# A recommendation tower on one Trainium2 core: the last chunk's late stage in two parts of two tiles

## The reference

```python
e = jnp.stack([tbl_0[ids[:, 0]], tbl_1[ids[:, 1]], ..., tbl_25[ids[:, 25]]], axis=1)   # (2048, 26, 128)
sd = jnp.einsum('bfd,bd->bf', sparse_values, dense_features)
ss = jnp.einsum('bfd,bgd->bfg', sparse_values, sparse_values)
pairs = ss[:, iu, ju]                                   # 325 pairs above the diagonal
z = jnp.concatenate([dense_features, sd, pairs], axis=1)
h = jnp.concatenate([z, r_dense_features], axis=1)      # 607 wide
h = jnp.maximum(h @ W_top1 + b_top1, 0.0)               # 512
h = jnp.maximum(h @ W_top2 + b_top2, 0.0)               # 256
y = h @ W_top3                                          # (2048, 1)
```

## Time and profile before

| what | value |
|---|---|
| median of three runs | 391.6 us (390.85 to 392.52) |
| the profiled execution | 391.02 us |
| its span, first to last instruction | 389.2 us |
| busy: PE, PE weight loads | 348.4 us (90%), 269.9 us (69%) |
| busy: DVE, ACT, POOL | 242.9, 190.6, 264.3 us |
| mean granted clock of TensorE | 0.952 |

### The profile page before, as it was taken

One profiled execution on the slowest core, in us unless ns is written; L12 is line 12 of the kernel. 1 busy time (PEld: TensorE's weight loads), 2 busy tenths in 40 slices (PEclk: granted clock), 3 DMA queues, 4 the chain that ended last, 5 costly groups with the idle time before them and its releaser, 6 DMA issues.

```text
span 389.2 us, 12471 instructions
## 1 busy us (share of the span) xinstructions
PE 348.4 (90%) x5471; PEld 269.9 (69%) x5471; DVE 242.9 (62%) x475; ACT 190.6 (49%) x299; POOL 264.3 (68%) x279
## 2 busy tenths in 40 slices
PE   2899985999999999999999989999999988346996
PEld 0566664877788877777788878776788876235773
DVE  0789996877888644887987446886986341101420
ACT  3356664768323337577143157674133169822333
POOL 6777775777777777777777777777777777771000
PEclk9999998999999998999999998999999989756899
DMA  7999212333333232343223222433431222220000
GB/s 189 247 233 216 49 47 93 89 86 88 112 85 81 83 74 62 90 99 105 85 84 105 78 61 52 117 90 90 110 80 54 54 56 58 57 53 20 3 0 0
DMA packets 20107, 33.41 MB, mean 86 GB/s; under 512 B 7916, under 2 KB 10488, under 8 KB 20055
## 3 DMA queue, kind: packets, MB, share of 16 engines
q0 software_dynamic: 8704, 17.84, 18.2%
q1 hardware_dynamic: 11351, 14.78, 14.3%
HBM read 32.60 MB, written 0.01 MB: 84 GB/s over the span
## 4 chain that ended last, share of the span: by engine, by line
PE 37%; POOL 8%; issue 4%; ACT 3%; DMA 1%; DVE 1%; POOLq 0%; ACTq 0%; DVEq 0%
PE late_bank L599 9%; POOL rows L498 8%; PE gram_bank L561 5%; PE turn_bank L542 3%; PE turn_bank L522 3%; PE turn_bank L523 3%; PE late_bank L522 2%; PE late_bank L523 2%; PE spare_bank L635 2%; ACT turned L349 2%; DMA rows<-in_tbl_dram,index 1%; PE gram_bank L635 1%; PE turn_bank L579 1%; PE late_bank L647 1%; PE gram_bank L579 1%
## 5 line engine op out<-in xcount | busy, mean ns | idle before, releaser
L498 POOL DMA_INDIRECT rows<-in_tbl_dram,index x272 | 263.5, 969 | 87.1 <-issue 79.5
L915 DVE TENSOR_TENSOR one_hot<-table_ids,row_number 125x512 fp32r<-125x512 int32 x216 | 134.4, 682 | 27.3 <-PE turn_bank L523 15.4
L349 ACT COPY turned<-turn_bank 128x512 f32<-128x512 f32 (+1 forms) x72 | 70.9, 1029 | 47.1 <-PE turn_bank L542 47.0
L542 PE MATMUL turn_bank<-ident,rows 128*128 128x128 f32 x288 | 48.2, 302 | 21.2 <-DMA rows<-in_tbl_dram,index 11.2
L522 PE MATMUL late_bank<-one_hot,table_hi 125*128 125x512 f32 x144 | 61.8, 429 | 0.9 <-DVE table_lo L996 0.9
L561 PEld LDWEIGHTS gram_bank<-turned 128*27 128x27 f32 x4096 | 46.9, 110 | 22.4 <-issue 19.9
L561 PE MATMUL gram_bank<-turned 128*27 128x26 f32 x4096 | 56.2, 197 | 5.8 <-issue 5.3
L542 PEld LDWEIGHTS turn_bank<-ident,rows 128*128 128x128 f32 x288 | 36.9, 155 | 31.4 <-issue 16.6
L523 PE MATMUL late_bank<-one_hot,table_lo 125*128 125x512 f32 x144 | 58.3, 405 | 0.0
L319 DVE COPY gram<-gram_bank 124x208 f32<-124x208 f32 x32 | 12.0, 374 | 59.3 <-PE gram_bank L561 59.0
L522 PE MATMUL turn_bank<-one_hot,table_hi 125*128 125x512 f32 x96 | 38.8, 404 | 1.0 <-DVE one_hot L913 1.0
(11 more groups left out here) (84 smaller groups left out, 400.9 us busy)
## 6 DMA issues: line engine op xcount, KB each, us to landing
table_ids<-in_ids_by_table_dram SPq DMA_DIRECT2D x27, 256.0 KB, 3.3
rows<-in_tbl_dram,index POOLq DMA_INDIRECT x272
turned<-in_tbl_dram SPq DMA_DIRECT2D x6, 448.0 KB, 13.7
looked_up<-in_tbl_dram SPq DMA_DIRECT2D x3, 448.0 KB, 6.5
rows<-in_r_dense_features_dram SPq DMA_DIRECT2D x16, 64.0 KB
gram<-in_W_top_dram SPq DMA_DIRECT2D x1, 702.0 KB
gram<-in_W_top_dram SPq DMA_DIRECT2D x1, 512.0 KB
turned<-in_tbl_dram SPq DMA_DIRECT2D x6, 52.0 KB
```

The source lines that it names most:

```text
L349: copy(to[:, f0:f1], of).then_inc(rows_copied[n % 2], 1)
L498: pool.indirect_dma_start(out=rows[:, row % RING_ROWS, :], out_offset=None, in_=tables[f], in_offset=bass.IndirectOffsetOnAxis(ap=index[:, ...
L542: last = pe.transpose(turn_bank[n % 2][:, f - f0, :], rows[:, (tile * ROWS + f) % RING_ROWS, :], ident[:])
L915: last = nc.vector.tensor_tensor(hot, table_ids[0:RK, (chunk.n * LOOKUPS + s) % ID_SLOTS, 0:wide], row_number[0:RK, k:k + 1].broadcast_to( ...
```

## The change

The last chunk's late stage is done in two parts, `EARLY` with tiles 12 and 13 and `FINAL` with tiles 14 and 15, each with 256 samples as its moving columns where there were 512. The number of instructions of the late stage doubles with that. `EARLY` is written between the products of tile 14 and the turns of tile 15. So that both can be in flight, `EARLY` has PSUM banks of its own (the spare bank, the bank of the row numbers, a late bank) and its own room for pairs and for `h2` in the half of `gram` that tiles 14 and 15 no longer need, since their products go where those of tiles 12 and 13 were. In the last chunk the odd row turns are copied by DVE and the even ones by ACT, where ACT copied all of them, and DVE places the looked-up rows of tiles 14 and 15. The output is stored in two parts. Chunks 0 to 2 keep their order. The core of the diff:

```diff
+EARLY = Part(LAST.n, LAST.first, HALF, 0)
+FINAL = Part(LAST.n + 1, LAST.first + HALF, HALF, HALF)
+PARTS = len(CHUNKS) + 1
...
+        half_room = HALF * GROUPS * LATER
+        early_pairs_room = late_room[:, half_room:half_room + GROUP * PAIRS]
+        half_h2 = late_room[:, half_room:half_room + N2 * HALF * P].rearrange("p (n b) -> p n b", n=N2)
+        last_y = late_room[0:1, half_room + N2 * HALF * P:half_room + N2 * HALF * P + CHUNK]
...
+        half_cols_bank = [spare_bank[:], row_number[:], late_bank[1][:], *free_bank[0:2], spare_bank[:], row_number[:]]
+        whole_pairs_bank = free_bank
+        half_pairs_bank = [bank[:, 0:HALF * P] for bank in (gram_bank[1], spare_bank, row_number)]
...
+        half_h2_bank = [spare_bank[:], row_number[:]]
...
+            room = n % (HALF * UNITS) if chunk is LAST else n
+            copy(gram[0:ACROSS, room * UNIT:(room + 1) * UNIT, :], of).then_inc(gram_copied[mine], 1)
...
+                if part.tiles == TILES:
+                    if g == 2 and part is not LAST:
+                        pe.wait_ge(found_copied, (part.n + 2) * LOOKUPS + LATE - 2)
+                    if g >= COLS_TURNS - 2:
+                        pe.wait_ge(cols_copied[0], part.n * COLS_STEPS[0] + g - (COLS_TURNS - 2) + 1)
+                else:
+                    if g == 0:
+                        pe.wait_ge(y_rows_copied, 1)
+                    if g >= COLS_TURNS - 2:
+                        pe.wait_ge(cols_copied[g - (COLS_TURNS - 2)], part.n * COLS_STEPS[g - (COLS_TURNS - 2)] + 1)
...
+                elif n == 1:
+                    pe.wait_ge(cols_copied[0], part.n * COLS_STEPS[0] + 2)
...
+            def work_off_last():
+                for t in range(HALF):
+                    for u in range(UNITS):
+                        turn_rows(LAST, t + 1, turns_before(u))
+                        products(LAST, t, u)
+                    if t == 0:
+                        turn_outputs()
+                turn_rows(LAST, 3, (0,))
+                dense_ahead(EARLY, 0)
+                for g in range(COLS_TURNS):
+                    turn_products(EARLY, g)
+                pe.wait_ge(cols_copied[1], EARLY.n * COLS_STEPS[1] + 2)
+                products(LAST, 2, 0)
+                for k in range(K_PAIRS):
+                    turn_pairs(EARLY, k)
+                turn_rows(LAST, 3, (1,))
+                pe.wait_ge(pairs_split, EARLY.n * K_PAIRS + 1)
+                products(LAST, 2, 1)
+                dense_ahead(EARLY, 1)
+                layer1(EARLY, 0)
+                turn_rows(LAST, 3, (2,))
+                layer1(EARLY, 1)
+                products(LAST, 2, 2)
+                layer2(EARLY, 0)
+                layer1(EARLY, 2)
+                turn_rows(LAST, 3, (3,))
+                products(LAST, 2, 3)
+                layer2(EARLY, 1)
+                layer1(EARLY, 3)
+                layer2(EARLY, 2)
+                layer2(EARLY, 3)
+                turn_rows(LAST, 3, (4,))
+                half_layer3(EARLY)
+                for u in range(UNITS):
+                    products(LAST, 3, u)
+                dense_ahead(FINAL, 0)
+                for g in range(COLS_TURNS):
+                    turn_products(FINAL, g)
+                for k in range(K_PAIRS):
+                    turn_pairs(FINAL, k)
+                dense_ahead(FINAL, 1)
+                for n in range(N1):
+                    layer1(FINAL, n)
+                    for k in LAYER2_AFTER[n]:
+                        layer2(FINAL, k)
+                layer2(FINAL, N1 - 1)
+                half_layer3(FINAL)
...
+            def work_off_last():
+                for t in range(HALF):
+                    for u in range(UNITS):
+                        copy_rows(act, LAST, t + 1, [g for g in turns_before(u) if g % 2 == 0])
+                        if u % 2:
+                            copy_products(act, LAST, t * UNITS + u)
+                        if u == 1 and t == 0:
+                            place_found(act, LAST, 1)
+                    if t == 0:
+                        copy_output_rows()
+                copy_rows(act, LAST, 3, (0,))
+                for g in range(1, COLS_TURNS, 2):
+                    copy_cols(act, EARLY, g)
+                for k in range(K_PAIRS):
+                    copy_pairs(EARLY, k)
+                copy_products(act, LAST, 2 * UNITS + 1)
+                relu1(EARLY, 0)
+                copy_rows(act, LAST, 3, (2,))
+                relu1(EARLY, 1)
+                relu1(EARLY, 2)
+                copy_products(act, LAST, 2 * UNITS + 3)
+                relu1(EARLY, 3)
+                for n in range(N2):
+                    relu2(EARLY, n)
+                copy_rows(act, LAST, 3, (4,))
+                copy_output(EARLY)
+                for u in range(1, UNITS, 2):
+                    copy_products(act, LAST, 3 * UNITS + u)
+                for g in range(1, COLS_TURNS, 2):
+                    copy_cols(act, FINAL, g)
+                for k in range(K_PAIRS):
+                    copy_pairs(FINAL, k)
+                for n in range(N1):
+                    relu1(FINAL, n)
+                for n in range(N2):
+                    relu2(FINAL, n)
+                copy_output(FINAL)
...
+            def work_off_last():
+                for t in range(HALF):
+                    for u in range(UNITS):
+                        copy_rows(dve, LAST, t + 1, [g for g in turns_before(u) if g % 2])
+                        if u % 2 == 0:
+                            copy_products(dve, LAST, t * UNITS + u)
+                        if u == 1 and t == 1:
+                            place_found(dve, LAST, 2)
+                    split_dense(LAST, t)
+                for g in range(0, COLS_TURNS, 2):
+                    copy_cols(dve, EARLY, g)
+                copy_products(dve, LAST, 2 * UNITS)
+                for k in range(K_PAIRS):
+                    split_pairs(EARLY, k)
+                copy_rows(dve, LAST, 3, (1,))
+                place_found(dve, LAST, 3)
+                split_h1(EARLY, 0)
+                split_h1(EARLY, 1)
+                copy_products(dve, LAST, 2 * UNITS + 2)
+                split_h1(EARLY, 2)
+                copy_rows(dve, LAST, 3, (3,))
+                split_dense(LAST, 2)
+                split_h1(EARLY, 3)
+                copy_products(dve, LAST, 3 * UNITS)
+                split_dense(LAST, 3)
+                copy_products(dve, LAST, 3 * UNITS + 2)
+                for g in range(0, COLS_TURNS, 2):
+                    copy_cols(dve, FINAL, g)
+                for k in range(K_PAIRS):
+                    split_pairs(FINAL, k)
+                for n in range(N1):
+                    split_h1(FINAL, n)
```

More of the change, by code:

```diff
@@ L52 @@
 TILES = 4
-SIZES = (4, 4, 4, 4)
+CHUNK_COUNT = 4
+HALF = TILES // 2
 CHUNK = TILES * P
@@ L98, with width, groups_in, samples_of @@
 SPREAD = 112
[L101 to L118, removed]
+Part = namedtuple("Part", "n first tiles at")
+CHUNKS = [Part(n, n * TILES, TILES, 0) for n in range(CHUNK_COUNT)]
+LAST = CHUNKS[-1]
+EARLY = Part(LAST.n, LAST.first, HALF, 0)
+FINAL = Part(LAST.n + 1, LAST.first + HALF, HALF, HALF)
+PARTS = len(CHUNKS) + 1
+def width(part):
+    return part.tiles * P
+def groups_in(part):
+    return part.tiles * GROUPS
+def samples_of(part):
+    return slice(part.at * P, (part.at + part.tiles) * P)
 def offset(row):
@@ L140, in turns_until, with blocks_before, blocks_after, hots_after @@
     return row // ROWS * TURNS + row % ROWS // TURN + 1
[L143 to L157, removed]
+def blocks_before(step):
+    return sum(BLOCKS.get(before, 0) for before in STEPS[:STEPS.index(step)])
+def blocks_after(*step):
+    return range(blocks_before(step), blocks_before(step) + BLOCKS.get(step, 0))
+def hots_after(*step):
+    blocks = blocks_after(*step)
     first = 0 if step == ("unit", 0, 0) else min(blocks.start + HOT_SLOTS, HOTS)
@@ L593, in turn_pairs, with add_layer1 @@
                 last.then_inc(pairs_turned, 1)
-            def add_layer1(chunk, n, k):
-                p, cols, wide = height(k), slice(n * P, (n + 1) * P), width(chunk)
+            def add_layer1(part, n, k):
+                p, cols = height(k), slice(n * P, (n + 1) * P)
                 for w, x in ((w1_hi, input_hi), (w1_hi, input_lo), (w1_lo, input_hi)):
-                    last = pe.matmul(h1_bank[n][:, 0:wide], w[0:p, k, cols], x[0:p, k, 0:wide],
+                    last = pe.matmul(h1_bank[n][:, 0:width(part)], w[0:p, k, cols], x[0:p, k, samples_of(part)],
@@ L658, in last_layer3, with turn_outputs @@
                 last.then_inc(y_summed, 1)
[L660 to L662 removed]
+            def turn_outputs():
+                pe.wait_ge(y_copied, LAST.n + 1)
                 pe.transpose(y_rows_bank, y[:], ident[:]).then_inc(y_turned, 1)
             def work_off(chunk, following):
[L668 to L671 removed]
+                for t in range(TILES):
@@ L799, in copy_output @@
                 else:
```

(6 more changed lines are left out.)

329 lines of the change are left out of this document (142 added, 187 removed).

## The result

The changed kernel takes 385.74 us, the median of six runs (383.97 to 387.31), where the kernel before took 391.77 (390.85 to 393.29, six runs beside them). The ratio is 0.9839, with an interval from 0.9803 to 0.9875: 1.6% faster. The forecast was 387.0, in a range from 383.0 to 391.5. The profiled execution took 384.49 us.

The account below looks back on a forecast made before the run. A gather-bound stretch with PE mostly idle, then 28.9 us of full PE work. The final part saves 9.7 us, 5.2 given back before it: span 384.7, 4.5 less; profiled execution 386.5, forecast 387.0, range 383.0 to 391.5.

Parts of the forecast that it names:

- The gather-bound stretch is filled: Tile 15's gathers: last stays at 351, early work fills PE's idle time, clock full from about 343.
- Tile 15's products start late by 5.2 us, at 360.5: Early part on PE, from 337.57: its work pushes the start of tile 15's products from 355.30 to 360.5.
- The wait for the fourth block: Early part, layer one's fourth block: PE idles 0.8 us for two ACT instructions and one on DVE.
- 256 columns at 0.127 us: Half-wide float32r matmuls: 0.107 of streaming plus 0.02 per instruction; bounds 0.117 and 0.233; 141 on the path.
- the rival that drew on such a sum: Half-wide matmuls over 0.15 us each; at 0.237, with weight loads not hidden, 402 us. Chance 0.14, no gain at all 0.03.
- Column turns with 64 weight columns at 0.075: Column turns of each half: 0.075 us each, between 0.06 and 0.117, and 0.15 at low clock.
- Products as long as before, with the idle stretch: Tile 15's products: 5.0 us as before, including 1.87 us of idle PE, ending at 365.5.
- A second stretch at low clock behind it, 1.3 us: Final part's dense matmuls and column turns: low clock after the products' idle stretch adds 1.3 us.
- The final part at 19.2 us: From the end of tile 15's products to the span's end: 19.2 us where the whole late stage cost 28.9.
- What costs nothing: Second store, issued about 20 us before the end, and shared row copies in tiles 13 and 14: no cost.
- the early part that comes too late: Tile 15's products wait behind the early part; no gain if they start later than 365.0, slower over 367. Chance 0.10.
- More than I say: First group 1.4 us earlier, matmuls at 0.117 (1.4 less), no second low stretch (1.3 less): 383 to 384.5. Chance 0.16.

Follow-up runs that it names:

- e4_again: Changed kernel with early column turns ahead of tile 15's first group, its fourth and fifth groups and half its products placed anew: 383.03 us, 0.9783 of before.
- e2_alone: Changed kernel with the early part's dense matmuls and column turns ahead of tile 15's first group: 385.08 us, 0.9876 of before.
- e1_alone: Changed kernel with both parts of the late stage behind tile 15's products: 672.22 us against 666.19 before the change, ratio 1.0089.
- e3_alone: Changed kernel with tile 15's last group and products between the early part's last layer blocks: 668.02 us against 672.01 before the change, ratio 0.9937.

## Why the prediction was right

It was right in direction and size: 387.0 was forecast and 385.74 measured, inside the forecast's own range. By its steps, in the profiled execution:

- **The gather-bound stretch is filled.** Right, with full clock from 342 (342.4 was said) and PE busy 17.2 of the 18 us from 342 to 360. But the last gather was not still at 351: it came at 352.32, and at 352.04 and 352.69 in `e4_again` and `e2_alone`, and in each trace one of tile 15's gathers took 1.6 to 1.7 us. That the change leaves the gathers alone was wrong by 1.3 us; what holds them up isn't known. PE came to the fourth group at 352.51, where about 353 was said, and it was luck that its rows, 1.3 us later than forecast, cost no wait.
- **Tile 15's products start late by 5.2 us, at 360.5.** Measured 359.71, 0.8 earlier. The first group was turned 0.6 earlier than before (336.98); its wait of 2.76 us for the DMA shows that this is set by gathers. The 69 early matmuls cost 0.7 less, the first turns and the dense matmuls behind them 0.2. Against that the column turns cost 0.9 more: they take 4.4 us, at 0.21 each until the clock rises and 0.106 behind it, where 0.15 and 0.075 were said. Some 0.2 are spread over the rest. The wait for the fourth block was 0.78 us, and 0.8 was said.
- **256 columns at 0.127 us.** This term was mis-sized, by 0.01 each: the rows stand 0.117 to 0.12 apart, so about 1.4 us on 141 matmuls. Of the 0.02 that I gave to each instruction at most half is there. The lower bound, half of the 0.233 at 512, was the truth. The Trainium skill, page "TensorE: Matmul & The Clock Gate", section "Back-to-back issue gap", gives 262 cycles for 256 columns, 109 ns at 2.4 GHz; the rows stand above that. It gives them for an isolated matmul, which the prediction doesn't say. Its "Part 3: Packing small matmuls" has weight loads overlap running matmuls only when the row group differs; no row of the changed kernel bears that out, with full-height matmuls 0.12 us apart, and the rival that drew on such a sum (0.237 each) is out.
- **Column turns with 64 weight columns at 0.075.** Wrong: the sixteen from 365.36 to 367.06 take 1.70 us, 0.106 each, so the bound of 0.117 was nearer. In the final part they delayed the pair turns to 368.21, 3.85 us behind its start, where 3.1 was said.
- **Products as long as before, with the idle stretch.** 4.65 us (359.71 to 364.36) where 5.0 was said; the idle stretch is 2.05 us, 1.87 before.
- **A second stretch at low clock behind it, 1.3 us.** It didn't come: the granted clock is 1.00 from 360 to 370, though PE idles for longer than it did before. The step that failed is that an idle stretch of that length brings the clock down by itself, read from the earlier trace rows alone. Before, PE had been busy for 8.5 of the 15 us ahead of the stretch (342 to 357), at the low clock nearly all that time; here it had worked for 17.2 of the 18 ahead. A third case speaks for this: in `e1_alone` the stretch of 2.06 us, with four of 0.8 to 1.1 us ahead of it, is followed by the low clock, though the clock had been full before:

```profile
618.00:630.00 12.00, 8.27 (x498) 6.89 (x500) 6.72 (x13) 4.31 (x7) 0.00 (x0) 1.00 0.02 5
632.00:635.00 3.00, 2.69 (x112) 2.56 (x113) 0.38 (x1) 0.33 (x1) 0.00 (x0) 0.50 0.02 5
```

  So the length of the idle stretch alone doesn't decide. That what PE did ahead of it does is the likeliest reading, and only argued; `e2_alone`, where PE had waited 3.75 us for gathers ahead of its own stretch, kept the full clock, so what exactly counts is open.
- **The final part at 19.2 us.** Measured 18.5: the clock 1.3 less, the matmuls 0.7 less, the columns 0.75 more, and 0.6 more of waits and restarts ahead of the second and the fourth block (378.60 stands 0.99 us behind the start of the matmul ahead of it). In sum the span ended 1.8 us below the 384.7 forecast, 1.1 of them ahead of the final part.
- **What costs nothing.** No wait in the trace is for the second store. Whether the row copies that DVE and ACT now share do anything wasn't tried alone.

Of the rivals, the early part that comes too late had its point at 365.0 and the products started 5.3 us ahead of it. "More than I say" named three items: 0.117 each, no second low stretch, and an earlier first group. The first two came in full, the third at 0.6 of 1.4 us, since the third gather of tile 15 was itself issued 0.6 later (334.16); the column turns took back about 1.6 of it. The right total is thus in part luck: 1.4 and 1.3 us too many in two terms stood against some 1.6 too few in the column turns.

The price of the split, which the prediction had only inside its sum, is now shown by itself: 36.0 us against 28.9 behind the products. It pays since 17.6 of these lie under gathers and push what follows by only 4.4.

## What to carry to other kernels

A stage that stands behind a stretch bound by transfers can be halved and one half put into that stretch. Price it by what both halves take with no cover (here 7 us more than the whole), by how far the inserted half pushes the last arrival's work, and by what is left at the end. Then read which wait is next before speeding up the inserted half: here it was the gathers again, and a warm clock 2.8 us earlier bought nothing until more of the half was put ahead of the later arrivals. Let dense runs of small instructions alternate with longer ones: one unit of 64 records at a time lost nothing, two in a row about 1 us.

## What the runs showed of the hardware

- Matmuls with 256 moving float32r columns stand half as far apart as those with 512 (0.117 to 0.12 and 0.233 us), with hardly a part per instruction to be seen. It is also about what a full weight load allows, so nothing here tells whether fewer columns would be faster still.
- Half the weight columns make a transpose hardly faster: 0.106 us with 64 and 0.117 with 128 at full clock.
- An idle stretch of 2.05 us left the granted clock at 1.00 in the kernel after, and one of 2.06 in `e2_alone` too; one of 2.06 in `e1_alone` was followed by 0.50, and so was one of 1.87 before.
- PE idles 1 to 2 us within runs of the small products, with nothing that it waits for, and the places are regular. In `e1_alone`, whose rows are above, 128 records stand between two such stretches, and in the kernel after 127 between those of 1.22 and 1.33 us, at 328.93 and 332.87; with a weight load for each record that is about 256 instructions. The Trainium skill, page "Runtime: NRT & Kernel Launch", section "Instruction fetch mechanics", says that instructions come in blocks of 256 and that crossing from one to the next is mostly hidden. The distance agrees, and so do the transfers of instructions in the kernel after (packets, MB, share):

```profile
q8 instruction: 44, 0.72, 0.8%
```

  That is 16 KB each, one for 254 of PE's 5585 matmuls and 5585 weight loads. That the crossing is hidden doesn't agree, by 0.9 to 2.1 us in these runs of small instructions; between longer matmuls it is hidden, as `e3_alone` shows. The page and the case fit each other, but no run changed the supply itself.
- On four of the chips every execution took 657 to 681 us, and elsewhere 381 to 394, but for one of the kernel before beside `e4_again`: 623.04. More than half of the extra time is idle stretches of another kind, with one to six records between them for 171 of the 219, 136 of 159.5 us. PE in order of time in `e1_alone`, tile 12:

```profile
591.13 0.20 PE L580 MATMUL gram_bank<-turned 128*27 128x26 f32 x1 [1.83 <-issue]
591.86 0.23 PE L580 MATMUL gram_bank<-turned 128*27 128x26 f32 x1 [0.53 <-issue]
```

  Blocks of 256 instructions don't explain these. The page's busy time by engine, in `e1_alone`:

```profile
PE 450.8 (67%) x5585; PEld 333.2 (50%) x5585; DVE 255.1 (38%) x504; ACT 185.3 (28%) x317; POOL 259.2 (39%) x279
```

The same line of the kernel after, on another chip:

```profile
PE 349.5 (91%) x5585; PEld 275.1 (72%) x5585; DVE 254.7 (67%) x504; ACT 184.4 (48%) x317; POOL 266.1 (69%) x279
```

The largest group of PE's waits in `e1_alone` (tile and line waiting, releaser: us in total, times, longest us):

```profile
PE gram_bank L580 <- issue: 159.5, 219, 2.6
```

And the same group in the kernel after:

```profile
PE gram_bank L580 <- issue: 5.3, 5, 2.0
```

PE is busy 101 us longer with as many instructions, at a mean clock of 0.76 where it was 0.973, and idles 154 us more in this one group; ACT and DVE work no longer than before. What sets such an execution apart isn't known.
